# Merging two expert blocks, reordering retention's last scatters, and moving a projection one row later in the delta rule

## The chip, the cores and the metric

The kernel runs on one core of one Trainium2 chip. The metric is the device time of one execution in microseconds (us); the median of three runs of the kernel before is 1981.84 us.

## The reference

The model has two layers over x of 32 sequences of 128 tokens with 128 features, all in fp32. Layer 0: a retention block (16 heads, group norm, output projection), then two mixtures of 8 experts, each token going to its best two. Layer 1: a softmax attention with a field term, a gated delta rule with 8 heads, a squared-ReLU MLP, a quaternion rotation and a quantized MLP. The parts that the change touches are these:

```
gate = softmax(x @ w_gate.T);  topk_scores, topk_idx = top_k(gate, 2)
out[token] = sum over its two experts of score * expert(x[token])        # twice: three-layer experts, then GELU experts
o = scan(delta rule) ; x = x + (rms_norm(o) * o_norm_w * silu(gate)) @ Wo
m = rms_norm(x);  y = square(relu(m @ W_fc)) @ W_proj;  x = x + y
```

## The kernel before, in words

The program is a row of stages. Each stage is one block in which the five engines run instruction streams of their own and meet at semaphores; at a stage's end all engines meet at a barrier, `Memory.release` (L52) clears the stage's semaphores on POOL (L54) and all meet again (L55).

**Retention** (`retention`, L376) handles the 32 sequences in 8 groups of 4, and carries the routing of the first experts behind it. In turn u of POOL's stream (the loop stands at the end of its section): the causal mask of the fourth score bank for the four sequences of group u (`mask`, L443), the root of the gate's mean square of group u-2 (`gate_root`, L452), the root of the group norm of group u-1 (`norm_root`, L448), and the scatters of group u-4 (`scatter`, L177: for each of 4 sequences two indirect DMAs of 128 rows to the tensor `pairs` in DRAM). A scatter of group q needs `placed` (the slots that DVE worked out, `gate_place`, L149 to L169) and `rows_kept` (ACT). DVE calls `gate_place(u-3)` in its turn u after the residual of group u-1 (L739). PE's `values` (L523) waits for a mask before it takes the scores of a sequence, and its `output` (L541) stands behind `values` of the third sequence.

**The two expert stages** (`experts_first` L1186, `experts_second` L1397) each take 39 tiles of 256 slots: SP loads a tile's rows with `load_pairs` (L820; the address is read from memory first), PE turns and multiplies, ACT applies the activation, DVE copies the expert's weights into a ring, POOL stores the results with indirect DMAs (L829). Between them, within the first stage, `combine_first` mixes the results, routes again with 64 scatters (L177), and `field_basis` works out a small table `fa` which SP stores (L1015). POOL waits for all scatters (`all_scattered`, L183) before the first stage's block ends (L1192).

**The delta rule** (`delta_rule`, L1985) walks over 32 rows (sequences). In the last 8, row k also carries group g = k-1 of the MLP (g from 0 to 6). PE's order in such a row: `invert` (L2325), `project_v` (L2340), `project_gate` (L2332), six waves of `solve` (L2358), between which stand `feed` (L2393, the up projection), `turn_output` (L2375) and two of the eight matmuls of `output` (L2382), then `mean_square` (L2397), `attend` (L2366), the rest of `output`, and last `project_back(g)` (L2406, the down projection: 4 accumulated fp32 matmuls of 512 columns, which the trace counts as 8 passes). DVE's order: `ct` (L2825), `scale_v` (L2716), `prepare(g)` (pieces of work on the weights of the last layer, L2751 to L2799), six waves (L2725), `inverse_mean_square(g)` (L2736, L2738), `og` (L2846), the residual (L2732), a reciprocal (L2855), and `keep_group(g)` (L2743, L2746), which reads PE's result and adds the sum that POOL made in `add_group` (L2650). ACT makes `ad` (L2577), `sv` (L2524), the gate (L2581) and the outputs' scale (L2534).

Of the kernel before, what the change touches and what calls it, by code (L numbers as in the profile page):

```python
# [6 lines left out]
B = 32  # L7
# [368 lines left out]
def retention(nc, w, c, dram, start_loads):  # L376
# [7 lines left out]
    with ExitStack() as ctx:  # L384
# [46 lines left out]
        with nc.Block() as block:  # L431
# [5 lines left out]
            def _(pool):  # L437
# [17 lines left out]
                for u in range(GROUPS + 4):  # L455
                    n, r, q = u - 1, u - 2, u - 4
                    if u < GROUPS:
                        mask(u, 0)
                    if 0 <= r < GROUPS:
                        gate_root(r)  # L460
                    if u < GROUPS:
                        mask(u, 1)
                    if 0 <= n < GROUPS:
                        norm_root(n)
                    if q == 0:
                        pool.wait_ge(c["filled"], 16 * FILLS)
                    for b in range(GB):
                        if 0 <= q < GROUPS:
                            scatter(nc, pool, g, dram, q, b)
                        if u < GROUPS and b in (0, 2):  # L470
                            mask(u, 2 + b // 2)
# [200 lines left out]
            def _(dve):  # L672
# [96 lines left out]
                for u in range(GROUPS + 2):  # L769
# [26 lines left out]
                    if more:  # L796
                        keep_q(u + 1)
                    if normed:
# [3 lines left out]
                    if 0 <= u - 3 <= GROUPS - 3:  # L802
# [35 lines left out]
def tiles_first(nc, m, w, c, dram, E2, loaded_2):  # L838
# [8 lines left out]
    h1 = m.sb("h1", [128, 2, HT, SLOTS])  # L847
    h2 = m.sb("h2", [128, 2, HT, SLOTS])
# [135 lines left out]
    return (banks + [xT_ps[0][:], xT_ps[1][:]], stored, YS), sync, tensor, scalar, vector, gpsimd  # L984
# [6 lines left out]
def field_basis(nc, m, w, c, dram, banks):  # L991
# [21 lines left out]
    def sync(sp):  # L1013
        sp.wait_ge(fa, 1)
        sp.dma_start(dram["fa"], e[:]).then_inc(stored, 16)  # L1015
        sp.wait_ge(stored, 16)
# [45 lines left out]
    return sync, tensor, scalar, vector  # L1062
# [16 lines left out]
def combine_first(nc, m, w, c, dram, loaded_2, banks, stored, YS):  # L1079
# [10 lines left out]
    field_sync, field_tensor, field_scalar, field_vector = field_basis(nc, m, w, c, dram, banks[0:4] + banks[5:6])  # L1090

    def gpsimd(pool):
# [3 lines left out]
        all_scattered(pool, g)  # L1096

    def sync(sp):
# [4 lines left out]
        sp.wait_ge(loaded_2, 16 * NE)  # L1103

    def tensor(pe):
# [25 lines left out]
        field_tensor(pe)  # L1131

# [21 lines left out]
    def vector(dve):  # L1154
# [25 lines left out]
        tile_tables(nc, ch, g, w, c)  # L1180
        field_vector(dve)

    return sync, tensor, scalar, vector, gpsimd


def experts_first(nc, w, c, dram, E2, loaded_2):  # L1186

    with ExitStack() as ctx:
        m = Memory(nc, ctx, "moe1")
        shared, tile_sync, tile_tensor, tile_scalar, tile_vector, tile_gpsimd = tiles_first(nc, m, w, c, dram, E2, loaded_2)  # L1190
        mix_sync, mix_tensor, mix_scalar, mix_vector, mix_gpsimd = combine_first(nc, m, w, c, dram, loaded_2, *shared)
        with nc.Block() as block:  # L1192
            @block.sync
            def _(sp):
                tile_sync(sp)
                mix_sync(sp)

            @block.tensor
            def _(pe):
                tile_tensor(pe)  # L1200
                mix_tensor(pe)

            @block.scalar
            def _(act):
                tile_scalar(act)
                mix_scalar(act)

            @block.vector
            def _(dve):
                tile_vector(dve)  # L1210
                mix_vector(dve)

            @block.gpsimd
            def _(pool):
                tile_gpsimd(pool)
                mix_gpsimd(pool)


def tiles_second(nc, m, w, c, dram):
    HT, XR, WR, AR, YS = 4, 4, 4, 6, 3  # L1220
    xg = m.sb("xg", [128, XR, 2, ROW])
    aim = m.sb("aim", [128, AR, 2], U32)
    mine = m.sb("mine", [128, 2, 2])
    one = m.sb("one", [128, NE, B])
    total = m.sb("total", [128, B])
    wt = m.sb("wt", [128, WR, PACKED])
    xT = m.sb("xT", [128, 2, SLOTS])
    h = m.sb("h", [128, 2, HT, SLOTS])
    y = m.sb("y", [128, YS, 2, D])
    xT_ps = [m.ps(f"xTp{i}", [128, GT]) for i in range(2)]  # L1230
    h_ps = [m.ps(f"hp{i}", [128, 2, SLOTS]) for i in range(4)]
    y_ps = [m.ps(f"yp{i}", [128, GB, D]) for i in range(2)]
# [106 lines left out]
def combine_second(nc, m, w, c, dram, turn_ps, stored, YS):  # L1339
    YR = 3  # L1340
    yt = m.sb("yt", [128, YR, GB, 2, D])
    rows = m.sb("rows", [128, 2, GB, D])
    x2T = m.sb("x2T", [128, 2, GT])
    none = m.sb("none", [128, GT])
# [52 lines left out]
def experts_second(nc, w, c, dram):  # L1397
    with ExitStack() as ctx:
        m = Memory(nc, ctx, "moe2")
        shared, tile_sync, tile_tensor, tile_scalar, tile_vector, tile_gpsimd = tiles_second(nc, m, w, c, dram)  # L1400
        mix_sync, mix_tensor, mix_vector = combine_second(nc, m, w, c, dram, *shared)
        with nc.Block() as block:
            @block.sync
            def _(sp):
                tile_sync(sp)
                mix_sync(sp)

            @block.tensor
            def _(pe):
                tile_tensor(pe)  # L1410
                mix_tensor(pe)

            @block.scalar
            def _(act):
                tile_scalar(act)

            @block.vector
            def _(dve):
                tile_vector(dve)
                mix_vector(dve)  # L1420

            @block.gpsimd
            def _(pool):
                tile_gpsimd(pool)
# [560 lines left out]
def delta_rule(nc, w, dram, x3, late, start_late, late_in):  # L1985
# [43 lines left out]
    with ExitStack() as ctx:  # L2029
# [88 lines left out]

        fc_ps = [x_ps[j // 2][:].rearrange("p h t -> p (h t)")[:, j % 2 * GT:(j % 2 + 1) * GT] for j in range(HT)]

        with nc.Block() as block:
# [141 lines left out]
            def _(pe):  # L2263
# [105 lines left out]
                def turn_output(r, i):  # L2369
                    pe.wait_ge(s["o_done"], r.n * 2 + i + 3)  # L2370
                    if i == 1:
# [992 lines left out]
```

## Time and profile before

| what | value |
|---|---|
| median of three runs | 1981.84 us (1981.5 to 1981.86) |
| the profiled execution, its own time | 1993.04 us |
| its span | 1990.9 us |
| TensorE clock over the span | 0.904 of full speed |
| busy PE / DVE / ACT / POOL | 82% / 63% / 54% / 44% |

The span is the stretch from the first to the last recorded instruction of the profiled execution. Positions in it are given in us from its start: retention takes 51 to 295, the first expert stage 296 to 571, the second 572 to 756, the attention up to about 1160, the delta rule up to 1893, and the last layer the rest. A time "idle before <- X" in brackets is what the engine waited just before the instruction, and what released it.

### The profile page before, as it was taken

What the parts mean: (1) busy time and instruction counts of PE and PEld (TensorE: products, weight loads), DVE (VectorE), ACT (ScalarE), POOL (GpSimd) and SP (SyncE); (2) the same over time, 40 slices, a digit from 0 to 9 for tenths busy, and PEclk for the clock granted to TensorE, in tenths of its full rate; (3) what the DMA queues carried; (4) which work ended last, traced back from release to release, by engine and by line L of the source; (5) the groups of instructions that cost most, each with busy time, mean ns of one, the idle gap of its engine ahead of it and who ended that gap; (6) DMA issues with size and microseconds to landing.
All of it is one profiled execution on the core that took longest, in us unless ns stands there. A gap on an engine that the chain in (4) does not pass through costs nothing. (4 is left out here: it accounts for less than half of the span.)

```text
span 1990.9 us, 43080 instructions
## 1 busy us (share of the span) xinstructions
PE 1642.5 (82%) x15379; PEld 1160.8 (58%) x15379; DVE 1258.4 (63%) x3287; ACT 1067.8 (54%) x3158; POOL 875.8 (44%) x1094
## 2 busy tenths in 40 slices
PE   0899719993359966999976899999999999899887
PEld 0354408982249953666645777777777776445533
DVE  7587634544344556887855767777777776466566
ACT  0353304441124424988943467777777777666543
POOL 0235654665546631443430876706244260622243
PEclk9997759995569976999988999999999999999988
DMA  2930014323112242000002322231222223120001
GB/s 66 397 108 23 26 42 120 107 71 118 39 53 71 74 137 99 33 21 26 24 28 77 83 63 64 58 77 39 75 51 72 60 54 82 44 51 30 16 12 42
DMA packets 157896, 136.14 MB, mean 68 GB/s; under 512 B 90005, under 2 KB 130262, under 8 KB 155542
## 3 DMA queue, kind: packets, MB, share of 16 engines
q1 hardware_dynamic: 148630, 115.09, 19.6%
q0 software_dynamic: 9088, 18.70, 2.9%
q8 instruction: 110, 1.80, 0.4%
q14 instruction: 68, 0.56, 0.1%
HBM read 77.17 MB, written 56.54 MB: 67 GB/s over the span
## 5 line engine op out<-in xcount | busy, mean ns | idle before, releaser
L829 POOL DMA_INDIRECT y<-moe_y,moe_aim x156 | 177.4, 1137 | 149.4 <-DVE moe_y L1322 62.7
L2725 DVE TENSOR_TENSOR delta_sv<-delta_sv,delta_zp 32x256 f32<-32x256 f32 x384 | 161.3, 420 | 118.6 <-PE delta_zp L2358 111.0
L1782 ACT ACTIVATE field_p<-field_sp,field_nm 128x128 f32<-128x128 f32 x512 | 180.3, 411 | 0.8 <-DVE field_nm L1866 0.7
L2642 POOL TENSOR_TENSOR delta_dd<-delta_dd,delta_prod 128x30 f32<-128x30 f32 (+11 forms) x270 | 154.8, 573 | 21.2
L2640 POOL TENSOR_TENSOR delta_prod<-delta_ll,delta_dd 128x30 f32<-128x30 f32 (+11 forms) x270 | 150.5, 557 | 21.2
L2635 POOL TENSOR_TENSOR delta_dd<-delta_ll,delta_minus 128x1024 f32<-128x1024 f32 (+1 forms) x9 | 24.2, 2687 | 298.4 <-DMA delta_ll<-lanes 298.4
L2358 PE MATMUL delta_zp<-delta_sv,delta_ct 128*32 128x128 f32 x1536 | 121.6, 279 | 11.3 <-DVE delta_sv L2725 10.9
L1782 ACT ACTIVATION_READ_ACCUMULATOR field_p<-field_sp,field_nm 128x1 f32 x512 | 128.4, 251 | 0.0
L2709 DVE SCALAR_TENSOR_TENSOR delta_la<-delta_xp,delta_ck,delta_dc 128x256 f32<-128x256 f32 x256 | 107.6, 476 | 5.9 <-PE delta_xp L2316 4.2
L2358 PEld LDWEIGHTS delta_zp<-delta_sv,delta_ct 128*32 128x32 f32 x1536 | 69.8, 109 | 70.3 <-DVE delta_sv L2725 35.8
L1294 ACT ACTIVATE moe_h<-moe_hp,moe_wt 128x256 f32<-128x256 f32 x156 | 64.1, 471 | 83.7 <-PE moe_hp L1267 83.7
L1876 DVE COPY field_pT<-field_ptp 128x512 f32<-128x512 f32 x128 | 84.0, 672 | 35.6 <-PE field_ptp L1646 35.6
L1866 DVE TENSOR_REDUCE field_nm<-field_sp 128x4 f32<-128x512 f32 x132 | 84.7, 684 | 13.7 <-PE field_sp L1639 13.7
L1646 PEld LDWEIGHTS field_ptp<-w_ident,field_p 128*128 128x128 f32 x512 | 59.0, 144 | 55.2 <-issue 44.1
L2534 ACT ACTIVATE delta_og<-delta_og,delta_rt 128x128 f32<-128x128 f32 x264 | 83.9, 390 | 12.4 <-DVE delta_rt L2855 12.4
L2280 PE MATMUL delta_xp<-delta_hk,w_dWk 128*128 128x128 f32 x384 | 86.4, 307 | 0.0
L177 POOL DMA_INDIRECT pairs<-moe_pairs,moe_index x64 | 63.0, 985 | 49.6 <-DVE moe_index L169 31.0
L1646 PE MATMUL field_ptp<-w_ident,field_p 128*128 128x128 f32 x512 | 77.9, 280 | 4.7 <-ACT field_p L1782 4.7
L928 ACT ACTIVATE moe_h<-moe_h1p,moe_wt 128x256 f32<-128x256 f32 x78 | 32.8, 471 | 86.1 <-PE moe_h1p L891 86.1
L2332 PE MATMUL delta_zp<-w_dWg,delta_hv 128*128 128x512 f32 x128 | 65.3, 633 | 16.3 <-ACT delta_sv L2524 16.3
L2316 PE MATMUL delta_xp<-w_x 128*32 128x256 f32 (+3 forms) x2048 | 77.5, 303 | 0.0
L1276 PEld LDWEIGHTS moe_yp<-moe_wt,moe_h 128*128 128x128 f32 x624 | 75.6, 192 | 2.0
(567 smaller groups left out, 4476.9 us busy)
## 6 DMA issues: line engine op xcount, KB each, us to landing
delta_al<-alpha SPq DMA_DIRECT2D x33, 512.0 KB
pairs<-c_none SPq DMA_DIRECT2D x16, 1032.0 KB, 16.4
moe_xg<-pairs SPq DMA_DIRECT2D x78, 129.0 KB
moe_yt<-y SPq DMA_DIRECT2D x16, 512.0 KB, 4.7
w_E<-in_E_dram SPq DMA_DIRECT2D x1, 4624.0 KB, 36.3
w_E<-in_E_dram SPq DMA_DIRECT2D x8, 578.0 KB
lanes<-delta_la SPq DMA_DIRECT2D x256, 16.0 KB, 1.5
delta_di<-inverses SPq DMA_DIRECT2D x64, 64.0 KB, 2.3
```

The lines of the kernel that those rows point to most:

```text
L829: nc.gpsimd.indirect_dma_start(results, bass.IndirectOffsetOnAxis(ap=aim[:, t % AR, j:j + 1], axis=0), y[:, t % YS, j, :], None).then_inc( ...
L1646: last = nc.tensor.transpose(pt_ps[i % 2][:, k, :], p[:, slot, i * HQ + k, :], w["ident"][:])
L1782: last = nc.scalar.activation(p[:, slot, h, :], s_ps[i][:, k, :], ACT.Exp, bias=nm[:, slot, h:h + 1], accum_out=zs[:, slot, h:h + 1])
L1866: nc.vector.tensor_reduce(nm[:, slot, i * HQ:(i + 1) * HQ], s_ps[i][:], AX.X, ALU.max, negate=True).then_inc(s["peak"], 1)
L1876: nc.vector.tensor_copy(pT[:, slot, i * HQ:(i + 1) * HQ, :], pt_ps[i % 2][:]).then_inc(s["pt_kept"], 1)
L2280: last = nc.tensor.matmul(ps[:, kind * T:(kind + 1) * T], w["dWq" if kind else "dWk"][:, h * T:(h + 1) * T], hk[:, p.half, :], start=True, ...
L2358: last = nc.tensor.matmul(z_ps[h // HH][g * BL:(g + 1) * BL, h % HH, :], ct[:, h, g * BL:(g + 1) * BL], sv[:, h, :], start=True, stop=True)
L2534: last = nc.scalar.activation(og[:, h, :], og[:, h, :], ACT.Identity, scale=rt[:, H + h:H + h + 1])
L2640: ch.link(nc.gpsimd.tensor_tensor(pr, ll[lanes, a, a + 1:].unsqueeze(2).to_broadcast([n, below, a]), dd[lanes, a, 0:a].unsqueeze(1).to_bro ...
L2642: last = nc.gpsimd.tensor_tensor(dd[lanes, a + 1:, 0:a], dd[lanes, a + 1:, 0:a], pr, ALU.subtract)
L2709: last = nc.vector.scalar_tensor_tensor(by_kind(la[:, p.slot, at(h), :]), by_kind(x_ps[i][:, j, :]), ck[:, at(h):at(h) + 1], dc[:, p.half, ...
L2725: nc.vector.tensor_tensor(sv[rows, two, :], sv[rows, two, :], z_ps[2 * pair // HH][rows, at, :], ALU.subtract).then_inc(s["z_kept"], 1)
```

## The change

Three edits, independent of each other.

1. Retention. In POOL's turns from u = 7 on, the two scatters of a sequence stand between the masks and roots instead of behind them: turn 7 is mask 0, `gate_root`, scatter 0, mask 1, `norm_root`, scatter 1, mask 2, scatter 2, mask 3, scatter 3; turn 8 is scatter 0, `gate_root`, scatter 1, `norm_root`, scatters 2 and 3; turn 9 has `gate_root` behind scatter 1. On DVE `gate_place` of group 5 (turn 8) stands ahead of the residual.
2. Experts. Both stages run in one block with shared tiles and banks; one barrier, one clearing of semaphores and one block end are gone. `all_scattered` moves from POOL to SP, the wait for the store of `fa` to the block's end, and the second stage's semaphores are cleared together with the first's.
3. Delta rule. `project_back(g-1)` stands in the next row, between `project_v` and `project_gate`; its result goes to the bank `w_ps` instead of `fc_ps[3]`. `inverse_mean_square(g-1)` stands ahead of `scale_v`, `keep_group(g-1)` behind it. For the last group (g = 6) all stays in its own row, with `inverse_mean_square` now behind the row's reciprocal. The two small products for the last layer (`turn_quaternions`, `turn_weights`) move along.

```diff
@@ retention, POOL
+                    if u >= GROUPS - 1:
+                        for b in range(GB):
+                            if u < GROUPS:
+                                mask(u, b)
+                            if b == 0 and u < GROUPS:
+                                gate_root(r)
+                            if b == 1 and u < GROUPS:
+                                norm_root(n)
+                            scatter(nc, pool, g, dram, q, b)
+                            if b == 0 and u == GROUPS:
+                                gate_root(r)
+                            if b == 1 and u == GROUPS:
+                                norm_root(n)
+                            if b == 1 and u == GROUPS + 1:
+                                gate_root(r)
+                        continue
@@ retention, DVE
+                    if u == GROUPS:
+                        gate_place(nc, dve, ch, g, c, u - 3, seen[:, 64:64 + 2 * GB * NE])
                     if normed:
                         residual(n)
...
-                    if 0 <= u - 3 <= GROUPS - 3:
+                    if 0 <= u - 3 < GROUPS - 3:
@@ combine_first
-        all_scattered(pool, g)
...
         field_sync(sp)
-        sp.wait_ge(loaded_2, 16 * NE)
+        sp.wait_ge(tabled, 1)
+        all_scattered(sp, g)
...
         field_tensor(pe)
+        pe.wait_ge(g["placed"], GROUPS)
+        pe.wait_ge(exps, 1)
...
         tile_tables(nc, ch, g, w, c)
+        dve.sem_inc(tabled, 1)
         field_vector(dve)
+        dve.wait_ge(loaded_2, 16 * NE)
@@ experts: one block, each engine in a row
+                sync_1(sp)
+                mix_sync_1(sp)
+                sync_2(sp)
+                mix_sync_2(sp)
+                field_stored(sp)
...
@@ delta_rule, PE
+        def result(g):
+            return w_ps[:].rearrange("p h t -> p (h t)") if g < RING - 2 else fc_ps[HT - 1]
...
-                def turn_output(r, i):
+                def turn_output(r, i, g=None):
                     pe.wait_ge(s["o_done"], r.n * 2 + i + 3)
+                    if i == 0 and g is not None and g > 0:
+                        pe.wait_ge(s["y_kept"], g)
...
                 def project_back(g):
                     pe.wait_ge(s["rl_kept"], g * HT + HT)
+                    if g < RING - 2:
+                        pe.wait_ge(s["x_kept"], (ROW_TURNS - 1) * RING + g + 2)
...
                     for i in range(2):
                         project_v(r, i)
+                    if g is not None and g > 0:
+                        project_back(g - 1)
+                    if g == 3:
+                        turn_quaternions()
+                    if g == 5:
+                        turn_weights()
...
-                    if g is not None:
+                    if g == RING - 2:
                         project_back(g)
@@ delta_rule, DVE
+                    if g is not None and g > 0:
+                        inverse_mean_square(g - 1)
                     scale_v(r)
...
+                    if g is not None and g > 0:
+                        keep_group(g - 1)
                     if g is not None:
                         prepare(g)
...
-                    if g is not None:
-                        inverse_mean_square(g)
...
-                    if g is not None:
+                    if g == RING - 2:
+                        inverse_mean_square(g)
                         keep_group(g)
```

## Rows read from the trace of the kernel before

**Rows 1.** The page's first part: busy time, share and instructions of each engine.
```profile
PE 1642.5 (82%) x15379; PEld 1160.8 (58%) x15379; DVE 1258.4 (63%) x3287; ACT 1067.8 (54%) x3158; POOL 875.8 (44%) x1094
```
**Rows 2.** Timeline of POOL in retention's end: start, us, engine, line, operation [idle before].
```profile
237.57 0.96 POOL L177 DMA_INDIRECT pairs<-ret_pairs,ret_index  x1 [0.30 <-issue]
240.74 1.04 POOL L452 TENSOR_TENSOR ret_rms<-ret_rms,ret_minus_half 128x4 f32<-128x4 f32 x1 [2.21 <-DVE ret_rms L744]
242.96 1.01 POOL L448 TENSOR_TENSOR ret_scale<-ret_scale,ret_minus_half 128x4 f32<-128x4 f32 x1 [1.18 <-DVE ret_scale L729]
...
255.99 1.04 POOL L452 TENSOR_TENSOR ret_rms<-ret_rms,ret_minus_half 128x4 f32<-128x4 f32 x1 [1.95 <-DVE ret_rms L744]
...
286.39 0.96 POOL L177 DMA_INDIRECT pairs<-ret_pairs,ret_index  x1 [0.30 <-issue]
```
**Rows 3.** Timelines of PE (first line) and DVE, same stretch.
```profile
229.96 1.08 PE L523 MATMUL ret_yp<-ret_pT,ret_vm 128*32 128x128 f32 x32 [2.55 <-POOL ret_pT L443]
...
233.54 0.69 DVE L739 TENSOR_TENSOR c_x1T<-ret_tb,c_x1T 128x512 f32<-128x512 f32 x1 [4.24 <-PE ret_tb L541]
...
237.83 0.17 DVE L169 TENSOR_SCALAR ret_index<-c_place 128x8 uint32<-128x8 f32 x1
```
**Rows 4.** Queue instructions by line, 562 to 573: xcount, ns min/median/max, first and last start.
```profile
L183 POOLq EVENT_SEMAPHORE  x1: 43/43/43, 564.4 to 564.4; - x1
...
L1192 POOLq DRAIN  x1: 5608/5608/5608, 564.6 to 564.6; - x1
```
**Rows 5.** Timeline of SP's DMA issues around three stage starts.
```profile
296.17 3.89 SPq L820 DMA_DIRECT2D moe_xg<-pairs  x4
...
564.42 0.32 SPq L1015 DMA_DIRECT2D fa<-moe_f_e  x1
571.97 15.17 SPq L820 DMA_DIRECT2D moe_xg<-pairs  x8
```
**Rows 6.** Queue instructions of L54: first stage's end (562 to 573), second's (752 to 758).
```profile
L54 POOLq EVENT_SEMAPHORE_RANGE_CLEAR  x1: 308/308/308, 570.6 to 570.6; - x1
...
L54 POOLq EVENT_SEMAPHORE_RANGE_CLEAR  x1: 178/178/178, 756.1 to 756.1; - x1
```
**Rows 7.** Timeline of PE in the last eight rows of the delta rule.
```profile
1722.77 3.60 PE L2406 MATMUL delta_xp<-delta_dc,w_late 128*128 128x512 f32 x8
...
1734.42 3.78 PE L2332 MATMUL delta_zp<-w_dWg,delta_hv 128*128 128x512 f32 x4 [4.23 <-ACT delta_sv L2524]
...
1756.68 1.98 PE L2325 MATMUL delta_xp<-delta_la,delta_di 32*32 32x224 f32 x64
...
1762.06 1.98 PE L2332 MATMUL delta_zp<-w_dWg,delta_hv 128*128 128x512 f32 x4 [1.48 <-ACT delta_sv L2524]
...
1778.02 3.60 PE L2406 MATMUL delta_xp<-delta_dc,w_late 128*128 128x512 f32 x8
1781.46 0.38 PE L2412 MATMUL delta_np<-delta_eye 128*128 128x128 f32 x2
...
1879.39 3.60 PE L2406 MATMUL delta_xp<-delta_dc,w_late 128*128 128x512 f32 x8
```
**Rows 8.** Busy time of stretches: length, PE, PEld, DVE, ACT, POOL, PE clock, DMA share, GB/s.
```profile
1735.00:1740.00 5.00, 5.00 (x9) 1.71 (x8) 1.24 (x6) 2.36 (x7) 0.00 (x0) 0.50 0.00 0
```
**Rows 9.** Timeline of DVE in the last eight rows.
```profile
1729.95 0.69 DVE L2746 TENSOR_TENSOR w_x<-w_x,delta_la 128x512 f32<-128x512 f32 x1 [2.78 <-POOL delta_la L2650]
...
1758.20 1.28 DVE L2825 TENSOR_TENSOR delta_ct<-delta_xp,w_offblock 128x512 f32<-128x512 f32 x2
...
1801.23 3.35 DVE L2738 RECIPROCAL delta_la<-delta_la 128x512 f32<-128x512 f32 x1
...
1812.31 1.77 DVE L2716 TENSOR_TENSOR delta_sv<-delta_sv,delta_kn 128x512 f32<-128x512 f32 x1 [2.56 <-ACT delta_sv L2524]
```
**Rows 10.** Timeline of PE, second wave of the rows with g = 3 and 6.
```profile
1790.98 0.63 PE L2358 MATMUL delta_zp<-delta_sv,delta_ct 128*32 128x128 f32 x8 [0.46 <-DVE delta_sv L2725]
...
1866.95 0.63 PE L2358 MATMUL delta_zp<-delta_sv,delta_ct 128*32 128x128 f32 x8 [1.10 <-DVE delta_sv L2725]
```
**Rows 11.** Timeline of POOL at the start of the row with g = 4.
```profile
1812.26 1.27 POOL L2650 TENSOR_TENSOR delta_la<-delta_la 128x512 f32<-128x512 f32 x1 [12.10 <-DMA delta_la<-x2T]
```

More of the change, by code:

```diff
@@ L983, in tiles_first @@
     banks = [ap.rearrange("p a b -> p (a b)") for ap in (h1_ps[0][:], h1_ps[1][:], h2_ps[0][:], h2_ps[1][:], y_ps[0][:], y_ps[1][:])]
-    return (banks + [xT_ps[0][:], xT_ps[1][:]], stored, YS), sync, tensor, scalar, vector, gpsimd
+    kept = {"xg": xg, "aim": aim, "mine": mine, "one": one, "total": total, "wt": wt, "xT": xT, "y": y, "hid": hid, "xT_ps": xT_ps, "h_ps": h1_ps + h2_ps, "y_ps": y_ps}
+    return kept, (banks + [xT_ps[0][:], xT_ps[1][:]], stored, YS), sync, tensor, scalar, vector, gpsimd
 FIELD = 0.3 * 0.7
@@ L1088, in combine_first @@
     weighed, mixed, turned, m_kept, lg_kept, chain = (m.sem("mix_" + s) for s in ("weighed", "mixed", "turned", "m_kept", "lg_kept", "chain"))
-    field_sync, field_tensor, field_scalar, field_vector = field_basis(nc, m, w, c, dram, banks[0:4] + banks[5:6])
+    (field_sync, field_sync_end, exps), field_tensor, field_scalar, field_vector = field_basis(nc, m, w, c, dram, banks[0:4] + banks[5:6])
+    tabled = m.sem("tabled")
     def gpsimd(pool):
@@ L1180, in vector, with tiles_second @@
         tile_tables(nc, ch, g, w, c)
+        dve.sem_inc(tabled, 1)
         field_vector(dve)
[L1183 to L1219, printed above, removed]
-    HT, XR, WR, AR, YS = 4, 4, 4, 6, 3
[L1221 to L1232, printed above, removed]
+        dve.wait_ge(loaded_2, 16 * NE)
+    return (yt, g["pairs"][:].rearrange("p a b c r -> p (a b c r)")), field_sync_end, sync, tensor, scalar, vector, gpsimd
+def tiles_second(nc, m, w, c, dram, kept):
+    HT, XR, WR, AR, YS = 4, 4, 4, 6, 3
+    xg, aim, mine, one, total, wt, xT, y = (kept[name] for name in ("xg", "aim", "mine", "one", "total", "wt", "xT", "y"))
+    xT_ps, h_ps, y_ps = kept["xT_ps"], kept["h_ps"], kept["y_ps"]
+    h = kept["hid"]
     gathered = [m.sem(f"gathered{i}") for i in range(XR)]
@@ L1336, in tiles_second, with combine_second @@
     return ([h_ps[0][:].rearrange("p a b -> p (a b)"), h_ps[1][:].rearrange("p a b -> p (a b)")], stored, YS), sync, tensor, scalar, vector, gpsimd
-def combine_second(nc, m, w, c, dram, turn_ps, stored, YS):
+def combine_second(nc, m, w, c, dram, yt, spare, turn_ps, stored, YS):
     YR = 3
[L1341 to L1344, printed above, removed]
+    rows = spare[:, 0:2 * GT].rearrange("p (n b d) -> p n b d", n=2, b=GB)
+    x2T = spare[:, 2 * GT:4 * GT].rearrange("p (n t) -> p n t", n=2)
+    none = spare[:, 4 * GT:5 * GT]
     loaded = [m.sem(f"loaded{i}") for i in range(YR)]
@@ L2405, in project_back @@
                     for j in range(HT):
-                        last = nc.tensor.matmul(fc_ps[HT - 1], w["Wproj"][:, j, :], f2[:, j, :], start=(j == 0), stop=(j == HT - 1))
+                        last = nc.tensor.matmul(result(g), w["Wproj"][:, j, :], f2[:, j, :], start=(j == 0), stop=(j == HT - 1))
                     last.then_inc(s["y_made"], 1)
@@ L2452, in step @@
                         if wave == 1:
-                            turn_output(before, 0)
+                            turn_output(before, 0, g)
                         if wave == 3:
@@ L3239, in program @@
                 place(layer0, EXPERTS_2)
-                experts_first(nc, w, c, dram, I["E2"], loaded_2)
-                experts_second(nc, w, c, dram)
+                experts(nc, w, c, dram, I["E2"], loaded_2)
             field_attention(nc, w, c, dram)
```

61 lines of the change are left out of this document (32 added, 29 removed).

## The prediction, made before the result was known

> **What bounds the kernel now.** I read the page first: PE is busy 82% of the span, no other engine over 63% [rows 1]. That is an average over stages with different limits, so the three edits have to be priced in their own stretches, and for each I read the timeline of the engine that the edit reorders.
>
> At retention's end the limit is POOL. From the last scatter of group 3 on, POOL issues the 32 scatters of groups 4 to 7, 1.27 us from start to start (0.96 busy, 0.30 of issue), and three roots; it is idle 2.21, 1.18 and 1.95 us, each time waiting for DVE to ask for a root, and ends with the scatter of 286.39 [rows 2]. DVE has its last work there done long before.
>
> Between the expert stages nobody computes. POOL sees the last scatter landed at 564.4, then stands in a drain of 5.61 us at the block's end; SP's first load of the second stage starts at 571.97 [rows 4, 5].
>
> In the last eight rows of the delta rule PE is nearly the limit: a plain row takes 24.9 to 25.1 us, and PE's largest pause in it is 1.48 us, before `project_gate`, waiting for ACT's `sv` [rows 7]. One row is odd: there the pause is 4.23 us, and the gate's matmuls take 3.78 us instead of 1.98, because the granted clock behind the pause is 0.50, the lower of its two levels, 1.2 GHz [rows 7, 8]. What made the pause is DVE: it stood 2.78 us in `keep_group(0)` for POOL's sum, with `ct` queued behind it [rows 9].
>
> **Edit 1, retention: -3.2 us.** Nothing is added or removed, only reordered. What goes is idle time of POOL: 2.21 + 1.18 + 1.95 = 5.34 us [rows 2], since ready scatters now fill it. What comes back: mask 1 and `norm_root` in turn 7 stand 2 x 1.27 = 2.5 us later. PE's `values` already waited 2.55 us for such a mask [rows 3], with `output` behind it in order, so the residual of 233.54 comes about 2.5 us later, and with it `gate_place`, whose last instruction (237.83) released the scatters of group 4. POOL is ready for them at 238.5, so it now idles up to 2.1 us there. Left: 5.34 - 2.1 = 3.2. The later roots find scatters in front of them; `gate_place` of group 5 ahead of the residual keeps group 5's scatters fed. Bounds: 5.3 if DVE makes up the delay, 0 if the roots come late enough to give all of it back. The last scatter's landing, the drain and the barrier behind it stay as they are.
>
> **Edit 2, experts: -6.3 us.** SP's queue becomes: store of `fa` (564.42, 0.32 long), a wait for `tabled` (set long before), the wait for the scatters (seen by POOL at 564.4), then the first load. Four loads with the reading of their addresses take 3.89 us, 0.97 each, about half of it the reading [rows 5]. So the first load starts at 564.74 + 0.6 = 565.4 instead of 571.97: -6.6. Behind it all moves together: DVE's weight copies no longer wait for the barrier and are done while the rows land, the table load of ACT too. The queued waits on PE (`placed`, `exps`) and DVE (`loaded_2`) are for things already there. POOL's drain goes to the end of the second stage, where POOL has stored its last tile long before SP's last store, and it is covered. Clearing costs 0.31 us at the first end and 0.18 at the second [rows 6]; together at the second end, so +0.3 there. Sum -6.3. Bounds: -5.6 (the drain alone) and -7.2 (nothing but the landing).
>
> **Edit 3, delta rows: -10.2 us.** PE's work stays the same; what counts is what it waits for. Take the start of a row's gate. Before: `project_back` of the row before takes 3.5 (1778.02 to 1781.46), then from `invert` to gate 5.38 (1756.68 to 1762.06), of it 1.48 pause [rows 7]: 8.9. Now `invert` and `project_v` take 3.9, then `project_back` 3.5: 7.4, if `sv` is there by then. It should be: without the reciprocal of 3.35 us in front of `og` [rows 9], DVE is at `ct` some 2 us after the start of `invert` (my estimate from the order of `og`, the root and its reciprocal), and from `ct` to the gate ACT's `ad`, table load and `sv` take 3.9 (1758.20 to 1762.06) [rows 7, 9], so `sv` is there at 5.9 and PE asks at 7.4. That is -1.48 a row.
> - Row with g = 1: its `invert` starts at 1722.77, its gate at 1722.77 + 7.4 = 1730.2 instead of 1734.42: -4.2. POOL's sum is there at 1729.95, before PE's result, so the 2.78 us wait goes too.
> - From that gate to the next before: 27.64 us (1734.42 to 1762.06), partly at the low clock. Now as in a plain row: 15.96 from gate to the row's end (1762.06 to 1778.02) plus 7.4, 23.4: -4.2.
> - The four rows with g = 3 to 6: 4 x 1.48 = -5.9.
> - Against it: DVE's `inverse_mean_square` (0.69 + 3.35) ends about 7.3 after `invert`'s start, `scale_v` 8.0, and two operations of 0.69 follow before `prepare`; this starts at 9.4, 2.0 behind the gate, where before only `scale_v` (0.69) stood between, 1.3 less. Where `prepare` is long, PE already paused 0.46 (g = 3) and 1.10 us (g = 6) for DVE's first wave [rows 10]; these grow by 1.3 each, and the other four rows get some 0.4 each: +4.2.
>
> Sum: -4.2 - 4.2 - 5.9 + 4.2 = -10.1; with rounding carried, -10.2. The two small products for the last layer stay on PE's path as before. Behind the last row `project_back(6)` (1879.39 before) keeps its place, and the tail is taken unchanged: the reciprocal, now behind the row's root, fits beside PE's output of the last row. SP's stores and loads of a row follow the residual, which comes earlier; no queue waits on the moved ones. Bounds: the low one is a DVE that eats the 1.48 of each row (-4), the high one is no added pause (-14).
>
> **A page against the trace.** DVE's `scale_v` took 1.77 us instead of 0.69 when it started 0.05 us behind POOL's sum of 1.27 us [rows 9, 11]: it ended about when that was over, plus its own time. By the Trainium skill, page "SBUF — State Buffer", section "Who interferes with whom", an operation of VectorE with two inputs in SBUF and one of GpSimd that reads SBUF exclude each other for their whole length. By that rule, the trace agrees. It speaks against this edit, since it moves more such operations of DVE to where POOL's sum runs; what it would make here is rival B.
>
> **The sum.** -3.2 - 6.3 - 10.2 = -19.7. The profiled execution took 1993.04 us (span 1990.9, 2.1 around it), 11 us or 0.6% above the median of the runs; the differences are too small for that ratio to matter. 1981.84 - 19.7 = 1962.1 us.
>
> **Rivals.**
> - A. DVE becomes the limit of the rows. With `inverse_mean_square` and `keep_group` ahead of the waves, each row's first wave waits, and 6 rows lose what the pause gave; only the odd row's gain of 4.2 from the clock stays. For it: 5.4 us of work in a new place. Against: the first wave has 1.3 us of room behind `scale_v`. 1981.84 - 3.2 - 6.3 - 4.2 = 1968.1.
> - B. POOL's sum falls on `scale_v` or `keep_group` in each of the six rows, 1.08 us each, 6.5 us in all. For it: the loads that the sum waits for come about 0.6 us later against `invert`, near `scale_v`. Against: part of it lies in room. 1962.1 + 6.5 = 1968.6.
> - C. Edit 2 doesn't do what it says: what the drain of 5.61 us stands for (writes under way) has to be waited for anyway, by the first gather. Then only barrier and clearing go: 1962.1 + 5.6 = 1967.7. Against: SP in the first stage already loads results without a drain after POOL's last store.
> - D. Slower. PE now waits in order at `turn_output` for `keep_group`. If that holds PE over four us in each row, the clock falls as in the odd row, where a pause of 4.23 did it, and a row costs 30.4 - 25.1 = 5.3 more. Five more rows: +26.5, no gain from edit 3: 1981.84 - 9.5 + 26.5 = 1998.8. It decides from a pause of about 4 us; the wait should be met 3 us before PE comes there.
> - E. Edit 1 gives nothing: 1965.3.
>
> **Chances.** Forecast 0.58; A 0.12; B 0.10; C 0.05; E 0.09; D 0.03; something unseen 0.03. Two executions of this kernel agree within 0.02%, so 0.2% (4 us) is what can be told from no change. Faster 0.95, same 0.02, slower 0.03. The range takes in A, B, C and E, and the high bounds of the three edits in part: 1956.0 to 1970.0.
>
> **What would show it.** Edit 1: last scatter at about 283 and no idle over 2.5 us on POOL before it. Edit 2: first load of the second stage about 1 us after the last scatter landed. Edit 3: gate starts 23.4 to 25 us apart, no pause before the gate, clock 1.00 in the row with g = 1, pauses of about 1.8 and 2.4 us behind the first wave with g = 3 and 6. Wrong would be: a pause before the gate, `low_made` (the end of `scale_v`) later than the first wave, or a clock below 1.00 in these rows.

## The result, and the profile after

| what | before | after |
|---|---|---|
| median of four runs each | 1981.85 us (1981.5 to 1984.12) | 1955.43 us (1952.46 to 1955.78) |
| the profiled execution, its own time / its span | 1993.04 / 1990.9 | 1955.78 / 1954.0 |
| TensorE clock over the span | 0.904 | 0.907 |

The ratio is 0.9865, with a 95% interval of 0.9848 to 0.9881: 26.8 us less (23.6 to 30.1). The forecast was 1962.1, 19.7 less, with a range from 1956.0 to 1970.0; the median lies 0.6 below it. A second comparison later gave 0.9889 (0.9868 to 0.9910), 22.0 us less; the mean of the two is about 24.

The page of after, first part. Busy times are as before [rows 1]; what shrank is idle time:
```profile
PE 1643.3 (84%) x15379; PEld 1163.1 (60%) x15379; DVE 1255.0 (64%) x3287; ACT 1067.0 (55%) x3158; POOL 875.8 (45%) x1094
```

**Retention.** Timeline of POOL (start, us, engine, line, operation, idle before), against [rows 2]:
```profile
223.05 1.04 POOL L452 TENSOR_TENSOR ret_rms<-ret_rms,ret_minus_half 128x4 f32<-128x4 f32 x1 [3.14 <-DVE ret_rms L758]
...
240.24 0.96 POOL L177 DMA_INDIRECT pairs<-ret_pairs,ret_index  x1 [1.33 <-DVE ret_index L169]
...
242.49 1.04 POOL L452 TENSOR_TENSOR ret_rms<-ret_rms,ret_minus_half 128x4 f32<-128x4 f32 x1
...
246.05 1.04 POOL L448 TENSOR_TENSOR ret_scale<-ret_scale,ret_minus_half 128x4 f32<-128x4 f32 x1
...
257.25 1.04 POOL L452 TENSOR_TENSOR ret_rms<-ret_rms,ret_minus_half 128x4 f32<-128x4 f32 x1
...
282.56 0.96 POOL L177 DMA_INDIRECT pairs<-ret_pairs,ret_index  x1 [0.30 <-issue]
```
The three roots no longer wait. What came back is 1.33 us at group 4's first scatter. From the root of turn 7 to the last scatter it is 59.5 us, where before has 63.9 (222.45 to 286.39).

**Between the expert stages.** Queue instructions of the wait for the scatters and of the block's end (xcount, ns, first and last start), against [rows 4]:
```profile
L183 SPq EVENT_SEMAPHORE  x2: 28/28/28, 538.7 to 548.8; - x2
...
L1389 POOLq DRAIN  x1: 11589/11589/11589, 700.8 to 700.8; - x1
```
And SP's timeline, against [rows 5]:
```profile
549.59 2.67 SPq L836 DMA_DIRECT2D moe_xg<-pairs  x3
```
SP sees the last scatter landed at 548.8 and loads 0.8 us later. The drain is now 11.6 us long, but it ends at 712.4, 20 us ahead of the block's end (732.5).

The merged block pays a little back at its end. POOL clears twice there, and from the stage's last matmul to the attention's first it is 8.5 us (8.4 to 8.6 in the kernels with edit 2, 7.7 to 7.8 in those without). Queue instructions in after, then PE in after and in before:
```profile
L54 POOLq EVENT_SEMAPHORE_RANGE_CLEAR  x2: 178/252/326, 732.8 to 733.4; - x2
```
```profile
728.25 1.11 PE L1352 MATMUL moe_h1p<-w_ident,moe_pairs 128*128 128x128 f32 x4 [1.34 <-DVE moe_pairs L1359]
736.74 1.22 PE L1607 MATMUL field_xa<-field_xT,w_WqT 128*128 128x512 f32 x1 [7.38 <-DMA field_xT<-x2T]
```
```profile
751.60 1.11 PE L1371 MATMUL moe_hp<-w_ident,moe_rows 128*128 128x128 f32 x4 [2.07 <-DVE moe_rows L1378]
759.34 1.22 PE L1609 MATMUL field_xa<-field_xT,w_WqT 128*128 128x512 f32 x1 [6.62 <-DMA field_xT<-x2T]
```

**The last eight rows.** Timeline of PE, against [rows 7] and [rows 10]:
```profile
1709.79 1.88 PE L2334 MATMUL delta_zp<-w_dWg,delta_hv 128*128 128x512 f32 x4
...
1732.80 1.88 PE L2334 MATMUL delta_zp<-w_dWg,delta_hv 128*128 128x512 f32 x4
...
1737.30 0.63 PE L2360 MATMUL delta_zp<-delta_sv,delta_ct 128*32 128x128 f32 x8 [1.02 <-DVE delta_sv L2733]
...
1749.84 1.72 PE L2327 MATMUL delta_xp<-delta_la,delta_di 32*32 32x224 f32 x64
1751.49 1.98 PE L2342 MATMUL delta_zp<-w_dWv,delta_hv 128*128 128x512 f32 x4
1753.31 3.60 PE L2412 MATMUL delta_wp<-delta_dc,w_late 128*128 128x512 f32 x8
...
1756.97 1.88 PE L2334 MATMUL delta_zp<-w_dWg,delta_hv 128*128 128x512 f32 x4
...
1761.30 0.63 PE L2360 MATMUL delta_zp<-delta_sv,delta_ct 128*32 128x128 f32 x8 [0.84 <-DVE delta_sv L2733]
```
From g = 1 on no gate waits any more (the gate with g = 0 still waits 2.40 us, as before). Instead PE pauses behind the first wave, for DVE: 1.02, 0.84, 0.39 and 1.38 us with g = 2, 3, 4 and 6.

**One stretch has nothing to do with the change.** In the profiled execution of before DVE stood idle 3.3 to 6.2 us at five places of the second routing, and the profile names no releaser ("remote"). ACT and PE waited with it; POOL went on issuing scatters every 1.27 us until it had none left, and then stood 5.81 and 7.61 us. Timelines of DVE (two of the five) and POOL there:
```profile
498.65 0.20 DVE L137 TENSOR_SCALAR moe_kept<-moe_gate_rest 128x32 f32<-128x32 f32 x1 [6.21 <-remote]
502.19 0.22 DVE L158 TENSOR_TENSOR_SCAN moe_upto<-moe_goes_on,moe_yp 128x32 f32<-128x32 f32 x1 [3.34 <-remote]
```
```profile
504.91 1.18 POOL L177 DMA_INDIRECT pairs<-moe_pairs,moe_index  x1 [5.81 <-DVE moe_index L169]
...
543.09 0.96 POOL L177 DMA_INDIRECT pairs<-moe_pairs,moe_index  x1 [7.61 <-DVE moe_index L169]
```
The 64 scatters there took 94.1 us (468.01 to 562.08); in the thirteen other profiled executions of this study, six of them of kernels with the old blocks, they took 81.3 to 82.1. That is some 12 us more, and this execution was 11 us above its median.

### The profile page after: what moved, and what is told of

It is laid out like the page before. It is cut to its first block and busy times, and to the rows that moved or that the text cites. A ratio compares the mean times of both kernels' runs of the same rounds, so it can differ in the third digit from the quotient of the medians.

```text
span 1954.0 us, 43075 instructions
## 1 busy us (share of the span) xinstructions
PE 1643.3 (84%) x15379; PEld 1163.1 (60%) x15379; DVE 1255.0 (64%) x3287; ACT 1067.0 (55%) x3158; POOL 875.8 (45%) x1094
## 5 line engine op out<-in xcount | busy, mean ns | idle before, releaser
L845 POOL DMA_INDIRECT y<-moe_y,moe_aim x156 | 177.5, 1138 | 142.6 <-DVE moe_y L985 63.0
L2360 PE MATMUL delta_zp<-delta_sv,delta_ct 128*32 128x128 f32 x1536 | 121.6, 279 | 14.2 <-DVE delta_sv L2733 13.7
L2542 ACT ACTIVATE delta_og<-delta_og,delta_rt 128x128 f32<-128x128 f32 x264 | 83.9, 390 | 11.6 <-DVE delta_rt L2865 11.6
L718 DVE TENSOR_TENSOR ret_pT<-ret_sp,w_causal 128x512 f32<-128x512 f32 x96 | 60.7, 681 | 26.8 <-PE ret_sp L528 26.4
L1637 PE MATMUL field_sp<-field_km,field_qT 32*128 32x512 f32 x264 | 75.8, 668 | 1.8 <-ACT field_p L1780 1.8
L944 ACT ACTIVATE moe_hid<-moe_h1p,moe_wt 128x256 f32<-128x256 f32 x78 | 32.8, 471 | 81.4 <-PE moe_h1p L907 81.4
L2575 ACT ACTIVATE delta_ad<-delta_zp 128x128 f32<-128x128 f32 x256 | 66.3, 289 | 19.4 <-PE delta_zp L2368 19.4
```

Of the source, the lines that this page charges most:

```text
L845: nc.gpsimd.indirect_dma_start(results, bass.IndirectOffsetOnAxis(ap=aim[:, t % AR, j:j + 1], axis=0), y[:, t % YS, j, :], None).then_inc( ...
L2360: last = nc.tensor.matmul(z_ps[h // HH][g * BL:(g + 1) * BL, h % HH, :], ct[:, h, g * BL:(g + 1) * BL], sv[:, h, :], start=True, stop=True)
L2542: last = nc.scalar.activation(og[:, h, :], og[:, h, :], ACT.Identity, scale=rt[:, H + h:H + h + 1])
```

## The experiments

Times are ratios to the kernel before, timed beside it on the same chip, in us of 1980. Three sets of before, 71 executions, spread from 1972.7 to 1989.6 there, so a time tells 3 us apart at best. Each kernel's profile tells more: in this table every interval is a difference of two starts in its one profiled execution. "Scatters" is from `gate_root` of turn 7 to retention's last scatter; "end" from there to the first tile's load; "second" from the last scatter of the second routing to the second stage's first load; "rows" the six intervals between the gates of g = 0 to 6; "tail" from the last gate to the next layer's first matmul. One profile is not exact either: e2_experts leaves retention as it was and has 67.1 instead of 63.9 there (its `norm_root` of turn 7 waited 3.44 us for DVE instead of 0.27), and e3_delta has 10.7 instead of 9.9 between the expert stages.

| kernel | us against before (95%) | scatters | end | second | rows | tail |
|---|---|---|---|---|---|---|
| before | | 63.9 | 9.8 | 9.9 | 155.5 | 31.3 |
| e1_retention | -4.9 (-8.1 to -1.8) | 58.6 | 9.9 | 9.9 | 151.6 | 29.9 |
| e1_pool | -4.2 (-7.9 to -0.6) | 60.8 | 9.8 | 9.9 | 151.3 | 29.9 |
| e2_experts | -6.5 (-8.9 to -4.4) | 67.1 | 9.8 | 3.1 | 153.9 | 29.9 |
| e3_delta | -15.6 (-19.8 to -11.7) | 63.9 | 9.9 | 10.7 | 142.6 | 29.1 |
| e3_tail | -2.8 (-5.7 to 0) | 63.9 | 9.8 | 9.9 | 154.0 | 28.9 |
| b_nodrain | -9.9 (-13.7 to -6.3) | 63.9 | 4.5 | 4.4 | 150.4 | 31.0 |
| b_spwait | +1.2 (-1.6 to +4.0) | 63.9 | 8.2 | 8.3 | 151.6 | 29.9 |
| after (first) | -26.8 (-30.1 to -23.6) | 59.5 | 9.8 | 3.1 | 140.6 | 29.1 |
| after_again | -22.0 (-26.1 to -17.8) | 59.6 | 9.8 | 3.1 | 141.0 | 29.4 |
| x_recip_old | -21.6 (-26.7 to -16.6) | 59.1 | 9.8 | 3.1 | 142.1 | 30.6 |
| x_early | +5.0 (+2.6 to +7.5) | 59.6 | 9.8 | 3.1 | 167.3 | 31.6 |
| x_between | -24.8 (-29.1 to -20.6) | 59.6 | 9.8 | 3.2 | 139.7 | 28.1 |
| x_best | -33.9 (-37.0 to -30.9) | 59.0 | 4.5 | 3.2 | 139.7 | 27.9 |

**The edits one at a time.** Each kernel is the one before with the hunks of one edit alone.

> Edit 1 alone. The forecast: 3.2 us faster than before (last scatter 3.2 earlier). Reading of the trace after: 3.5 us (its last scatter came 3.8 earlier, the second stage's first scatter 3.3). Rival: the reordering does nothing by itself, 0 us. Rival for the missing part of the sum: retention and what follows give 5 us or more.

> Edit 2 alone. The forecast: 6.3 us faster. Reading of the trace after: 6.8 us (last scatter's start to the second stage's first load 3.1 instead of 9.9 us). Rival: in the profiled execution of before all engines stood still twice in the second routing, some 12 us together, and in that of after not; if the merged block is what takes that away, this kernel gains about 19 us. If those stops belong to that one execution, it gains 6 to 7 and the stretch of the 64 scatters is as long in a new execution of before.

> Edit 3 alone. The forecast: 10.2 us faster. Reading of the trace after: from the gate with g = 0 to the end of the delta rule 17.0 us less than before, so this kernel should be 15 to 17 us faster. Rival: the edits help each other or the traces differ by chance, and this edit gives 10 us; then the other 6 us of the result must show in the two other kernels.

They add, within these intervals: 4.9 + 6.5 + 15.6 = 27.0, against 26.8 and 22.0 measured together. Edit 1's scatters are 5.4 us shorter (63.94 to 58.56), all of the idle time of [rows 2]. Edit 2's interval is 6.8 shorter, and the stop in the second routing wasn't there (82.0 us), nor in e1_retention (82.1), which keeps the old blocks: it belonged to that one execution. Edit 3 is worth more than the forecast's 10.2 by the time.

**Edit 1, split.** Kernel e1_pool is e1_retention without this:
```diff
+                    if u == GROUPS:
+                        gate_place(nc, dve, ch, g, c, u - 3, seen[:, 64:64 + 2 * GB * NE])
```


> Edit 1 without its part on DVE: POOL's new order, but gate_place of group 5 behind the residual of turn 8 as before. In the run of edit 1 alone that placing ended at 248.9 and POOL asked for it at 251.0; behind the residual it would end about 2.5 us behind 250.1, so POOL waits about 1.5 us there: last scatter 1.5 later than in the run of edit 1 alone, 3.9 us earlier than before. Rival: DVE's order doesn't matter, and the last scatter comes as early as there.

Timeline of POOL in e1_pool, group 5's first scatter:
```profile
253.14 0.96 POOL L177 DMA_INDIRECT pairs<-ret_pairs,ret_index  x1 [2.75 <-DVE ret_index L169]
```
The wait came where expected, 2.75 us instead of 1.5. So by the rows, of the 5.4 us 3.1 are POOL's order and 2.3 the one placing moved on DVE; the two times (-4.9 and -4.2) can't tell them apart.

**Edit 2: what the drain costs.** Two kernels from before, `Block(no_gpsimd_drain=True)` at retention's and the first experts' block, and the wait moved to SP:
```diff
-        with nc.Block() as block:
+        with nc.Block(no_gpsimd_drain=True) as block:      # b_nodrain, both blocks
...
-        all_scattered(pool, g)
+        all_scattered(sp, g)                               # b_spwait, at the end of SP's stream
```


> Kernel before with the drain of GpSimd left out at the end of two blocks, retention's and the first expert stage's (all scatters have been waited for ahead of both ends, as before); barrier and clearing stay. If the drain is what edit 2 saves, the first load of the second stage comes 5.6 us earlier behind the last scatter (9.9 to about 4.3 us), and retention's end to the first tile's load 9.8 to 4.5 us: 10.9 us faster in all. Rival C of the forecast: the writes under way have to be waited for all the same, by the barrier or the first loads: less than 3 us.

> Kernel before with the wait for all scatters moved from POOL to SP at the end of the same two blocks, so that POOL's drain starts right behind the last scatter, about 1.3 to 2.4 us earlier. If the drain is work of its own of 5.3 to 5.6 us, it overlaps the landing and each stage is up to 1.3 to 2.4 us shorter. Rival: the drain waits for the landing first and then takes its time, as that of 9.64 us at the second stage's end suggests: no change, or slower.

Without the drain each end is 5.3 to 5.5 us shorter and the kernel 9.9: the barrier and the loads behind it do not wait for anything in its place. Rival C is out. In b_spwait the drains read (queue instructions, ns, start):
```profile
L431 POOLq DRAIN  x1: 20431/20431/20431, 272.1 to 272.1; - x1
L1192 POOLq DRAIN  x1: 20744/20744/20744, 534.5 to 534.5; - x1
```
They begin with scatters still queued and end at 292.5 and 555.2, where 286.3 and 548.6 are the last scatters' starts: 6.3 and 6.6 behind them, where before has 7.9 (289.0 + 5.3 - 286.4) and 8.2. So by the rows the drain overlaps the landing in part, 1.6 us at each end, and the rest is its own. The time doesn't bear out the 3.2 us: it is +1.2, with an interval that begins at -1.6. In its profile the attention, the same in all kernels, took 303.1 us from its first matmul to the delta rule's, where the fourteen profiles lie between 297.1 and 303.1; whether that holds for its other nine executions isn't known, so a gain of the whole kernel by this edit is not shown.

**Edit 3: which part does it.** From after:
```diff
# x_recip_old: inverse_mean_square(g) back ahead of og in its own row, g = 0 to 5
-                    if g is not None and g > 0:
-                        inverse_mean_square(g - 1)
                     scale_v(r)
# x_early: project_back(g-1) ahead of invert
+                    if g is not None and g > 0:
+                        project_back(g - 1)
                     for i in range(2):
...
                         invert(r, i)
# x_between: keep_group(g-1) split over the first two waves
                         solve(r, wave)
+                        if g is not None and g > 0 and wave == 0:
+                            scale_group(g - 1)
+                        if g is not None and g > 0 and wave == 1:
+                            add_group_sum(g - 1)
```


> Kernel after with inverse_mean_square(g) back in its own row ahead of og (groups 0 to 5); project_back and keep_group stay moved. The forecast's mechanism: the 3.35 us reciprocal in front of og is what makes sv late, so the gate waits again, now 1.5 to 2 us a row, and rows take 24.9 us as in before: 9 to 11 us slower than after. Rival: what gains is that PE does project_back while it used to wait; then the gate waits less than 0.5 us and nearly all of the gain stays.

> Kernel after with project_back(g-1) ahead of the next row's invert instead of behind project_v. It must then wait for the residual, which reads the bank: in the trace after this ends 1.0 us behind PE's last output, so PE pauses 1.0 us in each of six rows, +6; the pauses behind the first wave (3.6 us in all) shrink by as much, so about 3 us slower than after in all. Rival: project_back's place behind project_v carries the gain (PE fills the wait for sv with it); then the gate waits for sv here as in before, and most of the gain of the rows is lost, 8 us or more.

> Kernel after with keep_group(g-1) split: its product of PE's result stands behind DVE's first wave, its sum behind the second, instead of both ahead of the first. If PE's second wave waits for DVE because this pair stands ahead of the first wave (1.02, 0.84, 0.39 and 1.38 us with g = 2, 3, 4 and 6 in the trace after), the pauses shrink to those of before (0 but for 0.46 at g = 3 and about 1.1 at g = 6 at most) and the kernel is 2 to 3 us faster than after; what could come back is 0.2 us a row at turn_output. Rival: DVE is full in any order, and the same microseconds show behind the second wave: no change.

> The changed kernel again, beside the same runs of before as the other three. Its first four runs gave a ratio of 0.9865. If the sum of the three edits alone (4.9 + 6.5 + 15.6 = 27.0 us, ratio 0.9864) is right, the same comes again; what the rows say without the clock (5.4 or 4.4, 6.8 and 11.6) is 23 to 24 us, ratio 0.988.

x_recip_old, PE: the gate follows project_back with no pause, though the reciprocal is in front of `og` again.
```profile
1729.89 1.72 PE L2327 MATMUL delta_xp<-delta_la,delta_di 32*32 32x224 f32 x64
1731.64 1.95 PE L2342 MATMUL delta_zp<-w_dWv,delta_hv 128*128 128x512 f32 x4
1733.44 3.60 PE L2412 MATMUL delta_wp<-delta_dc,w_late 128*128 128x512 f32 x8
1736.88 1.98 PE L2334 MATMUL delta_zp<-w_dWg,delta_hv 128*128 128x512 f32 x4
```
x_early, PE: the old pause is back, though the reciprocal is out of the way.
```profile
1732.83 3.67 PE L2412 MATMUL delta_wp<-delta_dc,w_late 128*128 128x512 f32 x8 [1.08 <-issue]
1736.43 1.72 PE L2327 MATMUL delta_xp<-delta_la,delta_di 32*32 32x224 f32 x64
1738.08 1.98 PE L2342 MATMUL delta_zp<-w_dWv,delta_hv 128*128 128x512 f32 x4
1741.55 1.98 PE L2334 MATMUL delta_zp<-w_dWg,delta_hv 128*128 128x512 f32 x4 [1.49 <-ACT delta_sv L2532]
...
1747.10 0.63 PE L2360 MATMUL delta_zp<-delta_sv,delta_ct 128*32 128x128 f32 x8 [1.48 <-DVE delta_sv L2733]
```
From `invert` to the gate it is 5.1 us here and 5.4 in before, of them 1.5 pause; in after 7.1, without one. The wait is for a chain that begins at `invert` (`ct`, `ad`, a table load, `sv`): in x_early DVE stands idle for `invert`'s result before `ct`. In after and x_recip_old DVE is still busy then. Timelines of `ct` on DVE in x_early; of `ct` and ACT's `sv` in after; and in x_recip_old, all with g = 2:
```profile
1737.52 1.45 DVE L2833 TENSOR_TENSOR delta_ct<-delta_xp,w_offblock 128x512 f32<-128x512 f32 x2 [4.03 <-PE delta_xp L2327]
```
```profile
1727.62 1.24 DVE L2833 TENSOR_TENSOR delta_ct<-delta_xp,w_offblock 128x512 f32<-128x512 f32 x2
1731.28 1.09 ACT L2532 ACTIVATE delta_sv<-delta_zp 128x512 f32<-128x512 f32 x2
```
```profile
1732.57 1.24 DVE L2833 TENSOR_TENSOR delta_ct<-delta_xp,w_offblock 128x512 f32<-128x512 f32 x2
1736.23 1.09 ACT L2532 ACTIVATE delta_sv<-delta_zp 128x512 f32<-128x512 f32 x2
```
Counted from `invert`'s start (1736.43, 1725.89 and 1729.89), `ct` starts 1.1, 1.7 and 2.7 us behind it. So the reciprocal in front of `og` does make `sv` later, by 0.95 us (6.34 instead of 5.39 behind `invert`). But PE, with `project_back` in front of the gate, comes there only after 6.9, and the gate starts at 6.99 instead of 6.91: the old place uses up the room and costs next to nothing at the gate. What edit 3 does is to put 3.4 us of PE's work behind `invert`, where this chain and DVE's longer one to the first wave run anyway. Ahead of `invert` the same 3.6 us, and the 1.1 to 1.4 for the residual, delay both chains: of these 4.8 a row, 4.4 show (167.3 against 140.6, six rows). I had expected 3 us in all; the rival was right, and even it named too little.

x_between, PE, the two rows where a pause is left, g = 3 and 6:
```profile
1768.28 0.63 PE L2379 MATMUL delta_wp<-w_ident,delta_og 128*128 128x128 f32 x4 [0.18 <-DVE w_x L2755]
...
1836.92 0.63 PE L2360 MATMUL delta_zp<-delta_sv,delta_ct 128*32 128x128 f32 x8 [0.33 <-DVE delta_sv L2733]
1837.73 0.63 PE L2379 MATMUL delta_wp<-w_ident,delta_og 128*128 128x128 f32 x4 [0.18 <-DVE w_x L2755]
```
The pauses of after (3.6 us) are 0.7. Its first interval of 24.6 us instead of 23.0 begins with a gate of 2.83 us instead of 1.98, behind the same pause of 2.40; the granted clock was 0.66 from 1693 to 1698. The whole 1.5 us lies there: the first pause for DVE comes 6.7 us behind this gate instead of 5.2. The five other intervals and the tail are 3.5 us shorter than in after. By time the gain over after is not shown (0.9875 against 0.9889, beside the same runs of before).

**The tail alone.**
```diff
-                    if g is not None:
+                    if g is not None and g < RING - 2:
                         inverse_mean_square(g)
...
                     nc.vector.reciprocal(rt[:, H:], rt[:, H:]).then_inc(s["rs_made"], 1)
+                    if g == RING - 2:
+                        inverse_mean_square(g)
```


> Kernel before with one thing moved: for the last group alone (g = 6) the mean square's reciprocal stands behind the row's own reciprocal instead of ahead of og. The forecast took the tail unchanged: 0 us. Reading of the trace after: from the last project_back to the first matmul of the next layer 11.78 us instead of 14.16, so 2.4 us faster, with the last output's sixteen matmuls at 2.05 instead of 3.48 us. Rival: the 2.4 us come from the clock that the rows before leave behind, and this kernel gains 1 us at most.

PE at the end of the delta rule, in before and then in e1_retention, which has the same code there:
```profile
1883.62 0.66 PE L2375 MATMUL delta_wp<-w_ident,delta_og 128*128 128x128 f32 x4 [0.62 <-ACT delta_og L2534]
1885.34 0.63 PE L2375 MATMUL delta_wp<-w_ident,delta_og 128*128 128x128 f32 x4 [1.07 <-ACT delta_oT L2528]
1886.65 3.48 PE L2382 MATMUL delta_wp<-delta_oT,w_dWo 128*128 128x128 f32 x16 [0.68 <-ACT delta_oT L2528]
```
```profile
1864.42 0.66 PE L2391 MATMUL delta_wp<-w_ident,delta_og 128*128 128x128 f32 x4 [0.62 <-ACT delta_og L2550]
1866.14 0.63 PE L2391 MATMUL delta_wp<-w_ident,delta_og 128*128 128x128 f32 x4 [1.07 <-ACT delta_oT L2544]
1867.45 2.05 PE L2398 MATMUL delta_wp<-delta_oT,w_dWo 128*128 128x128 f32 x16 [0.68 <-ACT delta_oT L2544]
```
Behind the same pauses the same sixteen matmuls take 3.48 or 2.05 us. Around them the granted clock was 0.62 (1886.0 to 1890.5 in before) and 1.00 (1867.0 to 1870.0 in e1_retention). By the rows the moved reciprocal takes away the wait of 0.62 and shortens the tail by 0.9 (28.9 against 29.9); the other 1.4 us of my reading were the clock, which differs from execution to execution.

**A version that beats both.** x_best is x_between with `no_gpsimd_drain=True` at retention's block.

> Kernel after with two things more: keep_group split between the first two waves as in x_between (by the rows 2 to 4 us), and retention's block ended without GpSimd's drain (5.3 us). Together 7 to 9 us faster than after: ratio to before 0.983 to 0.984. Rival: the drain has to be waited for anyway (3 us at most), or the split's gain isn't there: 0.986 or more.

1945.44 us median, ratio 0.9829 (0.9813 to 0.9844). Retention's end is 4.5 us instead of 9.8; rows and tail together are 2.1 us shorter than in after (167.6 against 169.7), in spite of a first interval of 24.6, again behind a slow gate (3.58 us). By the rows both terms are as expected. By the time it is 7.1 or 11.9 us faster than after, by which of its two measurements is taken; 7 to 9 was expected.

## Why the prediction was right or wrong

- **Edit 1, -3.2: the mechanism right, one term too large.** I let 2.1 us come back at group 4's scatter. It was 0 in e1_retention and e1_pool and 0.9 to 1.3 in the six others with the edit. In after the residual came 2.7 us later behind turn 7's root than before, as forecast, but the placing behind it only 0.9 later: DVE made up the rest. In e1_retention PE ran at full clock there (granted 1.00 against 0.50, `output` 1.12 us instead of 2.08), and the residual came only 0.9 later. Gain by rows 4.4 to 5.4.
- **Edit 2, -6.3: right.** 6.8 by the rows at the first stage's end, 5.5 of it the drain, less 0.7 at the second's end (two clearings, 0.6 us from start to start; I had +0.3): 6.1, and 6.5 by the time. Rival C would have left 5.6 of it undone and is refuted by b_nodrain.
- **Edit 3, -10.2: the mechanism right, three terms mis-sized.** In my own pair of profiles rows and tail shrank by 186.8 - 169.7 = 17.1. By intervals: -4.6 and -4.6 for the odd row and the one after it (forecast -4.2 each), then -0.7, -1.6, -1.3 and -2.0, tail -2.2. Three terms explain what is over 10.1. The pauses behind the first wave grew by 2.1 us, not 4.2 (1.0 with g = 2, 0.3 to 0.4 with g = 3, 4 and 6, 0 with g = 1 and 5): I had counted DVE's room too small. From `invert` to the gate it is 6.9 us, not 7.4 (1749.84 to 1756.97, less 0.23 for `turn_quaternions`): I had taken `invert` and `project_v` up to the end of the last matmul (3.9), but from start to start they are 3.5 where no pause follows, 0.45 us in each of six rows, 2.7. From the last `project_back` on it is 2.4 shorter (14.16 to 11.78), and I had left it unchanged, though the stall of 0.62 was in the trace; 0.9 of it is the moved reciprocal, 1.4 the clock. 10.1 + 2.1 + 2.7 + 2.4 = 17.3.
- **What the pair exaggerates.** In the five other profiled kernels with edit 3's code as before (e3_tail left out), rows and tail take 181.2 to 183.7, mean 181.8; in the three with edit 3 alone or all edits 169.7 to 171.6, mean 170.6. That is 11.3, or 12.1 with the first execution of before counted in. In four of the five the second interval is an ordinary 24.9, and the first 25.5 to 26.5: much of the 8.4 for the two was the low clock of one execution. In three of these four the gate with g = 0 had itself run slowly (2.84 to 3.50 us), POOL's sum was there in time, and the next gate waited 1.48 us and not 4.23. So -10.2 came near to the typical gain by errors that cancel: some 3 too much for the two rows (51.3 to 46.1 is 5.2), some 5 too little for `invert` to gate, pauses and tail.
- **The step that failed** is the sum of edit 3, by the size of its terms; that PE would fill the wait for `sv` held. The pauses behind the first wave, "+4.2", measured +2.1. "`invert` and `project_v` take 3.9, then `project_back` 3.5: 7.4" measured 6.9. "the tail is taken unchanged" put at nothing what measured -0.9, or -2.4 with the clock of this pair. So edit 3 measured 17.1 us in this pair and some 12.1 typically, instead of 10.2.
- **A condition that wasn't needed.** I made `sv`'s being in time depend on "without the reciprocal of 3.35 us in front of `og`". The times came out as estimated (`ct` 1.7 us behind the start of `invert`, against "some 2"). But x_recip_old has the reciprocal there and no pause at the gate; x_early hasn't, and has the pause. PE's order made nearly all of the gain; the reciprocal's move is worth 1.1 to 1.5 us in the rows (142.1 against the two executions of after), and by the time nothing that shows (-21.6 against -22.0). The tail of x_recip_old is 1.2 to 1.5 us longer too, but most of that is one group of matmuls that took 2.07 us instead of 1.12.
- **The sum.** By rows: 4.4 + 6.1 + 12.1 = 22.6, inside the second measured interval and 1.0 short of the first's edge (23.6). Forecast 19.7. Missing were 1.2 in edit 1 and 1.9 in edit 3, and edit 2 had 0.2 too much. The rest of the first result, 4 us, is within the spread of executions.
- **The range** was too narrow at its lower edge: I took 0.02% between two runs for the spread, and the errors of edits 1 and 3 go the same way. Seventy-one executions of before later ran from 1972.7 to 1989.6.
- **The rivals.** A, D and E didn't happen. B was there in kind: in after `scale_v` took 0.88 instead of 0.63 us at 1780.71, behind POOL's sum of 1779.77 to 1781.04, and 1.27 at 1732.76, behind that of 1732.22 to 1733.49; with g = 1, 3 and 5 `keep_group`'s second operation took 1.04 instead of 0.69 beside the sum. That is 1.9 us of DVE in six rows, where B had 6.5; how much of the pauses behind the first wave it makes wasn't separated. By the Trainium skill, page "SBUF — State Buffer", section "Who interferes with whom", two such operations exclude each other. The trace agrees: overlaps of 0.33 and 0.73 us cost 0.25 and 0.64. For D I had said that it decides from a pause of about 4 us. The traces don't bear that out: behind the same pause of 2.3 to 2.4 us the gate with g = 0 took 1.98 us in six profiles and 2.56 to 3.58 in the eight others.

## What to carry to other kernels

When an engine waits for a chain, find the instruction at which that chain starts, and put the engine's own movable work behind it: the same 3.4 us of PE made a row 4.4 us longer in front of `invert` than behind it, 1.1 to 1.4 of them its own wait for the residual. Look at every block end that follows indirect DMAs for GpSimd's drain; where their completion has been waited for already, leaving it out gave 5.3 and 5.5 us here. And base a forecast on typical intervals: the profiled execution of before had some 12 us of standstills and 5 us of low clock that others don't have.

## What was not expected of the hardware

- GpSimd's drain at a block's end took 5.30 and 5.61 us after 64 scatters that had all landed, within 0.01 us in every kernel with those ends, 9.62 to 9.64 at the second stage's end and 11.6 at the merged one's, but 1.1 to 2.0 us in four other blocks. What it depends on wasn't tried.
- Standstills of DVE, ACT and PE with no releaser in the profile, which made the second routing some 12 us longer, in one of fourteen profiled executions; POOL went on as long as it had scatters. Their cause is open.
- TensorE granted the lower clock behind the same pause in one execution and not in another (3.48 or 2.05 us for sixteen matmuls behind 0.68 us; 1.98 or 2.56 to 3.58 us for a gate behind 2.3 to 2.4), so single profiles differ by 5 us in these rows with the same code. The attention, untouched, differs by 6 us between profiles (297.1 to 303.1). How much of the spread of 17 us between executions of before either makes wasn't traced.
